# The four overhanging key columns of attention: the product with V issued over 128 rows instead of 4

## The chip, the cores and the metric

The kernel runs on one core of one Trainium2 chip. The metric is device time in microseconds (us), the median of several runs. TensorE (PE) multiplies matrices; VectorE (DVE), ScalarE (ACT) and GpSimd (POOL) work on rows; SyncE (SP) issues DMA transfers.

## The reference

The block is a half feed-forward, attention, and another half feed-forward, on x of 8 batches x 512 tokens x 256. Only attention matters here. Everything is float32:

```python
q, k, v = heads(x @ Wq), heads(x @ Wk), heads(x @ Wv)     # 16 heads of 64
k = concatenate([mem_k, k]); v = concatenate([mem_v, v])  # 4 memory keys ahead
dots = einsum('bhid,bhjd->bhij', l2norm(q), l2norm(k)) * 10
dots = einsum('hg,bgij->bhij', W_pre_th, dots)            # heads are mixed
dots = where(causal, mask_value, dots)
vk = top_k(dots, 64)[0][..., -1:]
dots = where(dots < vk, mask_value, dots)                 # the 64 largest stay
attn = softmax(dots)
attn = einsum('hg,bgij->bhij', W_post_th, attn)           # heads are mixed again
out = einsum('bhij,bhjd->bhid', attn, v) * head_scale * sigmoid(x @ Wg + bg)
x = x + out @ Wo
```

A row of `dots` has 516 columns: four memory keys and 512 tokens. So the keys that a tile of 128 queries can see are a whole number of 128-column blocks plus four more columns.

## The kernel before

Attention is `attention_phase`. A **tile** t is 128 queries; a batch has four tiles (TPB = 4), so there are 32. A tile is worked in 16 **groups** n of 8 queries: 8 queries x 16 heads fill 128 partitions, and a group's width in columns grows from 12 to 516 over the batch. Every engine walks its own hand-written list in steps of two groups (n0 = 0, 2, 4, ...), and semaphores tie the lists together.

What happens to group n, by engine:

- PE `score` makes the products of queries and keys, ACT copies them to SC (L1242), SP moves them by DMA to raw, PE `mix(n)` multiplies with mixpre (L1037), ACT `evict(n)` copies to S (L1253, L1256).
- POOL masks (L1388), ACT counts (L1263), POOL makes the threshold `minus_thr` (L1397), DVE `row_max` applies it (L1510) and `select_pair` picks the 64th largest and zeroes the rest of E (L1523 to L1568).
- POOL makes R from mixpost and rinv (L1413). PE `turn(n)` multiplies E with R (L1053) three steps later (LAG = 6 groups), ACT `out_PT(n)` copies the result to PT (L1289).
- Once a half tile u (64 queries, 8 groups) is there, PE `attend(u, pairs)` multiplies V with PT (L1079, one product for each head and each block of 128 keys), pair by pair of heads.

**The tail.** Behind the last whole block stand the four overhanging key columns. Only the second half tile (hh = 1) needs them, and of it the last eight queries. `turn` makes them at the last group of a tile (L1059, a result of 4 partitions), `out_PT` copies them to PTtail (L1294, 4 x 128), and `attend` adds for each of the 16 heads one product of 4 rows of V and 4 x 8 of PTtail (L1085).

**Where the tails stand in PE's list.** PE works the tails of tile t during tile t+1, second half: at g = 8 three pairs of heads, at g = 10 three, at g = 12 two. Ahead of the first stands `project(t - 1)` (L1099). The last tile's 16 heads come in one piece at the end, ahead of the last two projections. Each pair's list reads: L1079 products (1 to 4 blocks, two heads), L1085 products (two heads), next pair.

V has five slots of 128 keys in its ring. The four rows of the tail are the first four of slot t+1, which holds the keys of the next tile. A product in float32 shows in the trace as two LDWEIGHTS and two MATMUL records, so L1085's 512 products are 1024 records. The two heads of a pair write partitions 0 to 63 and 64 to 127.

Of the kernel before, what the change touches and what calls it, by code (L numbers as in the profile page):

```python
# [11 lines left out]
H, DH, MEM, TOPK = 16, 64, 4, 64  # L12
CYCLES = 3
P = 128
TPB = N // P
TILES = B * TPB
IG = 8
# [694 lines left out]
def attention_phase(nc, W, token_weights, a, x_dram, out_dram, again):  # L712

    with ExitStack() as c:
        def sb(name, shape, dtype=F32):
            return c.enter_context(nc.sbuf_tensor(name, shape, dtype))

        def sem(name):
            return c.enter_context(nc.semaphore(name))
# [3 lines left out]
        V = sb("V", [P, TPB + 1, HD])  # L723
# [36 lines left out]
        flag = sb("flag", [P, B])  # L760
        R = [sb(f"R{i}", [P, P]) for i in range(RBUFS)]
        PT = [sb(f"PT{i}", [P, TPB, H, HALF]) for i in range(2)]
        PTtail = sb("PTtail", [MEM, H, IG])

        def bank(name):
            return c.enter_context(nc.psum_tensor(name, [P, 512], F32))
# [5 lines left out]
        bankT = bank("bankT")  # L772
# [35 lines left out]
        rn_ready = sem("rn_ready")  # L808
        qk_ready = sem("qk_ready")
        halo = sem("halo")  # L810
        tk = sem("tk")
        flagged = sem("flagged")
        flag_sum = sem("flag_sum")
# [38 lines left out]
        def slot(j):  # L852

            return j % (TPB + 1)
# [55 lines left out]
        def wait_read(eng, *u):  # L910

            eng.wait_ge(D_read, max(place[x] for x in u) + 1)
# [54 lines left out]
        def _(pe):  # L967
# [95 lines left out]
            def attend(u, pairs):  # L1063
                t, hh = divmod(u, 2)
                if pairs[0] == 0:
                    pe.wait_ge(PT_out, (u + 1) * IG)
                    if t % TPB == 0:
                        pe.wait_ge(mem_in, 16 * (t // TPB + 1))
                        wait_read(pe, ("v", t, 1))
                    if hh:  # L1070
                        wait_read(pe, ("w", t, 1) if t == NT - 1 else ("v", t + 1, 1))
                    if u:
                        pe.wait_ge(gated, u)
                blocks = t % TPB + 1
                for pair in pairs:
                    for jb in range(blocks):
                        for lo in range(2):
                            h = 2 * pair + lo
                            last = nc.tensor.matmul(bankM[64 * lo:64 * lo + 64, pair * HALF:(pair + 1) * HALF],  # L1079
                                                    V[:, slot(t - blocks + 1 + jb), h * DH:(h + 1) * DH], PT[u % 2][:, jb, h, :],  # L1080
                                                    start=jb == 0, stop=jb == blocks - 1, skip_group_check=True)
                    if hh:
                        for lo in range(2):
                            h = 2 * pair + lo
                            last = nc.tensor.matmul(  # L1085
                                bankM[64 * lo:64 * lo + 64, (pair + 1) * HALF - IG:(pair + 1) * HALF],
                                V[0:MEM, slot(t + 1), h * DH:(h + 1) * DH], PTtail[:, h, :],
                                start=False, stop=True, skip_group_check=True)
                if pairs[-1] == PAIRS - 1:
                    last.then_inc(attended, 1)  # L1090
# [19 lines left out]
            for n0 in range(0, NG + LAG, 2):  # L1110
                t, g = divmod(n0, GPT)
# [47 lines left out]
                if t and g % 8 < 6:  # L1159
                    attend(2 * t - 2 + g // 8, ((0, 1, 2), (3, 4, 5), (6, 7))[g % 8 // 2])  # L1160
            attend(NU - 1, range(PAIRS))
            project(NT - 2)
            project(NT - 1)
# [4 lines left out]
        def _(act):  # L1168
# [113 lines left out]
            def out_PT(n):  # L1282
                t, g = divmod(n, GPT)
                u = n // IG
                act.wait_ge(turned, n + 1)
                if n % IG == 0 and u >= 2:
                    act.wait_ge(attended, u - 1)
                blocks, at = t % TPB + 1, n % IG * IG
                last = nc.scalar.copy(PT[u % 2][:, 0:blocks, :, at:at + IG],  # L1289
                                      bankC[n % 2][:, 0:blocks * P].rearrange("p (j h i) -> p j h i", h=H, i=IG))  # L1290
                if g == GPT - 1:
                    if t:
                        act.wait_ge(attended, 2 * t)
                    last = nc.scalar.copy(PTtail[:, :, :], bankT[0:MEM, 0:P].rearrange("p (h i) -> p h i", i=IG))  # L1294
                last.then_inc(PT_out, 1)

            xT(0)
# [6 lines left out]
            for n0 in range(0, NG + LAG, 2):  # L1304
                t, g = divmod(n0, GPT)
# [24 lines left out]
                if n0 >= LAG:  # L1330
                    out_PT(n0 - LAG)
                    out_PT(n0 + 1 - LAG)
# [26 lines left out]
        def _(pool):  # L1359

            def ln_rstd(j):
                pool.wait_ge(xn_stats, j + 1)
                nc.gpsimd.tensor_tensor(rstd[:, :], mv[:, 1:2], W.neghalf[:, 0:1], ALU.pow).then_inc(xn_rstd, 1)

            def copy_halo(j):

                dst = xnT[j % 2][:, :, 0:MEM]
                if j >= 2:
                    wait_read(pool, ("v", j - 2, 1))
                if j == 0:  # L1370
                    nc.gpsimd.memset(dst, 0.0).then_inc(halo, 1)
                else:
                    wait_read(pool, ("xT", j - 1, 0))
                    nc.gpsimd.tensor_copy(dst, xnT[1 - j % 2][:, :, P:P + MEM]).then_inc(halo, 1)

            def norm(j, i):
                pool.wait_ge(ssq_done, 2 * j + i + 1)
                nc.gpsimd.tensor_tensor(rn[:, i, :], ssq[:, i, :], W.neghalf[:, 0:H], ALU.pow).then_inc(rn_ready, 1)  # L1378
                pool.wait_ge(rn_ready, 2 * j + i + 1)
                wait_read(pool, ("qk"[i], j, 1))  # L1380
                v = qk[:, i, :].rearrange("p (h d) -> p h d", d=DH)
                nc.gpsimd.tensor_tensor(v, v, rn[:, i, :].unsqueeze(2).to_broadcast([P, H, DH]),
                                        ALU.mult).then_inc(qk_ready, 1)
# [31 lines left out]

            ln_rstd(0)
            copy_halo(0)
            norm(0, 0)
            norm(0, 1)
            ln_rstd(1)  # L1420
            for n0 in range(0, NG + LAG, 2):
                t, g = divmod(n0, GPT)
# [1039 lines left out]
def build(nc, a, out):  # L2462


    x1_dram = nc.dram_tensor("x1", ((TILES + 1) * P, D), F32, kind="Internal").ap()
    x2_dram = nc.dram_tensor("x2", (TILES * P, D), F32, kind="Internal").ap()
    rows = "b n d -> (b n) d"
    with ExitStack() as ctx:
        W = Weights()
        place_weights(nc, ctx, W)  # L2470
        names = ("Wq", "Wk", "Wv", "Wg")
        token_weights = [ctx.enter_context(nc.sbuf_tensor(n, [P, 2, HD], F32)) for n in names]
        with nc.sbuf_tensor("X_first", [P, TILES, D], F32) as X, ExitStack() as own:
            place_wide_weights(nc, own, W, "first", a)
            setup = Setup(nc, own, W, {**a, "x": a["x"].rearrange(rows)}, x1_dram)
            ffn_phase(nc, "ffn1", X, W, None, x1_dram, setup,
                      [(w[:, :, :], a[n].rearrange("(k p) n -> p k n", p=P)) for w, n in zip(token_weights, names)])
        again = ctx.enter_context(nc.sbuf_tensor("again", [P, B], I32))
        attention_phase(nc, W, token_weights, a, x1_dram, x2_dram, again)
        redo_phase(nc, W, token_weights, a, x1_dram, x2_dram, again)  # L2480
        with nc.sbuf_tensor("X_last", [P, TILES, D], F32) as X, ExitStack() as own:
            ffn_phase(nc, "ffn2", X, W, x2_dram, out.rearrange(rows), reload=place_wide_weights(nc, own, W, "last", a))
# [31 lines left out]
```

## Time and profile before

| | us |
|---|---|
| median of 3 runs | 2308.27 |
| lowest, highest | 2300.52, 2308.93 |
| span of the profiled execution | 2304.0 |
| PE busy in it | 2083.4 (90%) |
| DVE busy | 1767.9 (77%) |
| ACT busy | 1605.5 (70%) |
| POOL busy | 930.2 (40%) |

The profiled execution's own time is its span, first to last instruction, 2304.0; it lies 4.3 below the median of the three runs and between the lowest and the highest. Busy shares are averages over the whole span: the feed-forward parts take a little over 200 us at its start and as much at its end, and attention with its eight batches lies between. In the rows below, a time is counted from the span's start, a duration in square brackets at a row's end is idle time just before it with what ended it, and `x4` is a count of records.

### The profile page before, as it was taken

How to read it: one execution, taken by the hardware profiler on the slowest of the kernel's cores; microseconds unless marked ns; L12 is line 12 of the kernel's file. 1: busy time of each engine (PE TensorE's matmuls, PEld its weight loads, DVE VectorE, ACT ScalarE, POOL GpSimd, SP SyncE). 2: the span in 40 equal slices, each digit the busy share in tenths (PEclk: the TensorE clock that was granted, in tenths of full speed). 3: DMA queues.
4: the chain of work that ended last, by engine and by line, in shares of the span. 5: the costliest groups of instructions: out<-in, count | busy, mean ns of one | idle time of the engine just before them, and what ended most of it. 6: DMA issues, size and time to landing. Idle time of an engine off the chain costs nothing. (4 is left out here: it accounts for less than half of the span.)

```text
span 2304.0 us, 55635 instructions
## 1 busy us (share of the span) xinstructions
PE 2083.4 (90%) x16059; PEld 1351.7 (59%) x16060; DVE 1767.9 (77%) x6818; ACT 1605.5 (70%) x4676; POOL 930.2 (40%) x2738
## 2 busy tenths in 40 slices
PE   7995799989999999899989998999899989974997
PEld 3433456666666666666666666666666666663433
DVE  6565389958996899689968995899589958983446
ACT  4442589858985898689858976897689768851543
POOL 3001454444544554555455435543554355321000
PEclk9997799999999999999999999999999999997998
DMA  6002112111211121112111211121112101212002
GB/s 179 0 0 87 24 39 62 44 26 44 62 44 26 44 62 44 26 44 62 44 26 44 62 44 26 44 62 44 26 44 62 44 24 45 68 28 88 1 0 73
DMA packets 113219, 104.72 MB, mean 45 GB/s; under 512 B 34448, under 2 KB 110864, under 8 KB 112912
## 3 DMA queue, kind: packets, MB, share of 16 engines
q1 hardware_dynamic: 108000, 96.65, 16.5%
q10 hardware_dynamic: 4912, 4.46, 0.6%
q8 instruction: 134, 2.20, 0.4%
q14 instruction: 173, 1.42, 0.2%
HBM read 19.14 MB, written 12.71 MB: 14 GB/s over the span
## 5 line engine op out<-in xcount | busy, mean ns | idle before, releaser
L1053 PE MATMUL bankC<-R,E 128*128 128x128 f32 x2560 | 349.0, 286 | 39.5 <-POOL R L1413 39.4
L1053 PEld LDWEIGHTS bankC<-R,E 128*128 128x128 f32 x2560 | 335.6, 200 | 76.7 <-POOL R L1413 43.8
L1037 PE MATMUL bankB<-raw,mixpre 128*128 128x76 f32 (+37 forms) x1024 | 353.6, 433 | 18.9 <-DMA raw<-SC 18.6
L1388 POOL TENSOR_TENSOR S<-S,diagmask 128x8 f32<-128x8 f32 x512 | 114.2, 227 | 493.3 <-ACT S L1253 435.3
L1253 ACT ACTIVATE S<-bankB,aim_first 128x68 f32<-128x68 f32 (+56 forms) x456 | 231.5, 512 | 116.3 <-PE bankB L1037 115.6
L1510 DVE TENSOR_SCALAR_CACHE_REDUCE S<-S,minus_thr 128x68 f32<-128x68 f32 (+56 forms) x456 | 217.6, 514 | 110.1 <-POOL minus_thr L1397 109.5
L1564 DVE SCALAR_TENSOR_TENSOR E<-S,limit,E 128x68 f32<-128x68 f32 (+56 forms) x456 | 242.6, 567 | 35.4 <-ACT E L1279 6.3
L1413 POOL TENSOR_SCALAR R<-mixpost,rinv 128x128 f32<-128x128 f32 x512 | 187.5, 379 | 137.2 <-DVE rinv L1568 136.7
L1279 ACT ACTIVATE E<-S,nmax 128x12 f32<-128x12 f32 (+56 forms) x512 | 241.3, 533 | 0.0
L1079 PEld LDWEIGHTS bankM<-PT,V 128*64 128x64 f32 x5120 | 177.7, 137 | 101.1 <-issue 90.5
L1026 PE MATMUL bankD<-KT,QT 64*64 64x132 f32 (+8 forms) x2304 | 190.5, 405 | 51.2 <-ACT SC L1242 25.7
L1037 PEld LDWEIGHTS bankB<-raw,mixpre 128*128 128x128 f32 x1024 | 159.4, 191 | 118.8 <-issue 81.9
L1079 PE MATMUL bankM<-PT,V 128*64 128x64 f32 x5120 | 226.3, 229 | 0.9 <-DVE gate L1494 0.9
L1289 ACT COPY PT<-bankC 128x512 f32<-128x512 f32 (+3 forms) x512 | 193.9, 431 | 35.3 <-PE bankC L1053 30.3
L1271 ACT ACTIVATE junk_side<-S 128x68 bf16<-128x68 f32 (+56 forms) x456 | 199.5, 445 | 13.1 <-DVE S L1510 13.1
L1538 DVE MATCH_REPLACE8 near<-top,near 128x68 f32<-128x68 f32 (+56 forms) x456 | 199.5, 443 | 0.0
L1263 ACT ACTIVATE junk_first<-S 128x60 bf16<-128x60 f32 (+56 forms) x456 | 197.3, 444 | 0.3
L1378 POOL TENSOR_TENSOR rn<-ssq,neghalf 128x16 f32<-128x16 f32 x64 | 187.5, 2930 | 12.2 <-DVE ssq L1486 12.0
L1533 DVE MAX8 top<-near 128x8 f32<-128x68 f32 (+56 forms) x456 | 186.9, 449 | 0.3
L1542 DVE MAX8 top<-near 128x8 f32<-128x68 f32 (+56 forms) x456 | 186.3, 447 | 0.3
L1242 ACT COPY SC<-bankD 128x136 f32<-128x136 f32 (+7 forms) x256 | 165.8, 647 | 22.4 <-PE bankD L1026 20.5
L1528 DVE TENSOR_SCALAR near<-S,flip 128x68 int32<-128x68 int32 (+56 forms) x456 | 155.6, 381 | 8.2
(177 smaller groups left out, 3915.0 us busy)
## 6 DMA issues: line engine op xcount, KB each, us to landing
X_first<-in_L_attn_x_dram ACTq DMA_DIRECT2D x8, 512.0 KB, 10.1
x<-X_first SPq DMA_DIRECT2D x8, 512.0 KB, 2.9
xt<-x SPq DMA_DIRECT2D x32, 128.0 KB, 2.4
x<-xt SPq DMA_DIRECT2D x32, 128.0 KB, 2.5
X_last<-x SPq DMA_DIRECT2D x8, 512.0 KB, 6.7
out_dram<-X_last SPq DMA_DIRECT2D x8, 512.0 KB, 2.8
raw<-SC SPq DMA_DIRECT2D x8, 258.0 KB, 3.0
raw<-SC SPq DMA_DIRECT2D x8, 254.0 KB, 3.4
```

The source lines that it names most:

```text
L1026: last = nc.tensor.matmul(bankD[cols, r, i * s[3]:(i + 1) * s[3]], QT[rows, pair, HALF * hh:HALF * hh + HALF], KT[rows, pair, first:first ...
L1037: last = nc.tensor.matmul(bankB[n % 2][:, 0:wide(n)], W.mixpre[:, :], raw[n % RAWS][:, 0:wide(n)], start=True, stop=True)
L1053: last = nc.tensor.matmul(bankC[n % 2][:, jb * P:(jb + 1) * P], E[n % EBUFS][:, jb * P:(jb + 1) * P], R[n % RBUFS][:, :], start=True, stop ...
L1079: last = nc.tensor.matmul(bankM[64 * lo:64 * lo + 64, pair * HALF:(pair + 1) * HALF], V[:, slot(t - blocks + 1 + jb), h * DH:(h + 1) * DH] ...
L1253: nc.scalar.activation(S[n % SBUFS][:, 0:wide(n)], src, ACT.Identity, bias=W.aim_first[:, group(n)]).then_inc(S_out, 1)
L1263: nc.scalar.activation(junk_first[n % 2][:, 0:w], S[n % SBUFS][:, 0:w], ACT.Sign, scale=-1.0, accum_out=below[:, col(n)]).then_inc(below_d ...
L1271: nc.scalar.activation(junk_side[n % 2][:, 0:w], S[n % SBUFS][:, 0:w], ACT.Sign, accum_out=signs[:, col(n)]).then_inc(signs_done, 1)
L1279: nc.scalar.activation(E[n % EBUFS][:, 0:w], S[n % SBUFS][:, 0:w], ACT.Exp, bias=nmax[:, col(n)]) \
L1289: last = nc.scalar.copy(PT[u % 2][:, 0:blocks, :, at:at + IG], bankC[n % 2][:, 0:blocks * P].rearrange("p (j h i) -> p j h i", h=H, i=IG))
L1510: nc.vector.tensor_scalar(row, row, minus_thr[:, col(n)], None, ALU.add, ALU.max, accum_out=rmax[:, col(n)]).then_inc(max_done, 1)
L1538: at[n] = step(nc.vector.match_replace(out=row, in_to_replace=top[n % 2][:, 8 * r - 8:8 * r], in_values=row, imm_value=-FMAX))
L1564: at[n] = step(nc.vector.scalar_tensor_tensor(out=E[n % EBUFS][:, 0:w], in0=S[n % SBUFS][:, 0:w], scalar=least, in1=E[n % EBUFS][:, 0:w], ...
```

## The change

PTtail gets 128 partitions instead of 4. POOL fills it with zeros once, before the first tile. ACT goes on writing its first four partitions, and waits for the zeros at the first tile. The tail's product is issued with all 128 rows of V's slot and all 128 of PTtail. Rows 4 to 127 of PTtail are never written again, so they add zero times a value of V. The number of products and of records is the same, and so is their order.

```diff
-        PTtail = sb("PTtail", [MEM, H, IG])
+        PTtail = sb("PTtail", [P, H, IG])
...
+        tail_rows_zero = sem("tail_rows_zero")
...
                             last = nc.tensor.matmul(
                                 bankM[64 * lo:64 * lo + 64, (pair + 1) * HALF - IG:(pair + 1) * HALF],
-                                V[0:MEM, slot(t + 1), h * DH:(h + 1) * DH], PTtail[:, h, :],
+                                V[:, slot(t + 1), h * DH:(h + 1) * DH], PTtail[:, h, :],
                                 start=False, stop=True, skip_group_check=True)
...
                     if t:
                         act.wait_ge(attended, 2 * t)
-                    last = nc.scalar.copy(PTtail[:, :, :], bankT[0:MEM, 0:P].rearrange("p (h i) -> p h i", i=IG))
+                    else:
+                        act.wait_ge(tail_rows_zero, 1)
+                    last = nc.scalar.copy(PTtail[0:MEM, :, :], bankT[0:MEM, 0:P].rearrange("p (h i) -> p h i", i=IG))
...
             ln_rstd(0)
             copy_halo(0)
+            nc.gpsimd.memset(PTtail[:, :, :], 0.0).then_inc(tail_rows_zero, 1)
             norm(0, 0)
```

The only list with a row more is POOL's, at the start of attention. Before, behind the last table of the set-up:

```order
L624 TENSOR_TENSOR spread<-spread,half 128x1
L77 UNCONDITIONAL_BRANCH
L1358 UNCONDITIONAL_BRANCH
L1363 TENSOR_TENSOR rstd<-mv,neghalf 128x1
L1371 MEMSET xnT 128x2x4
L1378 TENSOR_TENSOR rn<-ssq,neghalf 128x16
L1382 TENSOR_TENSOR qk<-qk,rn 128x1024
```

And now, with the lines shifted by the new ones:

```order
L1361 UNCONDITIONAL_BRANCH
L1366 TENSOR_TENSOR rstd<-mv,neghalf 128x1
L1374 MEMSET xnT 128x2x4
L1421 MEMSET PTtail 128x128
L1381 TENSOR_TENSOR rn<-ssq,neghalf 128x16
L1385 TENSOR_TENSOR qk<-qk,rn 128x1024
```

The fill of PTtail stands between the fill of xnT's first columns and the first norm; PE's list has the same products in the same order as before.

## Rows read from the trace of the kernel before

**Rows 1.** The page, busy time of each engine.
```profile
PE 2083.4 (90%) x16059; PEld 1351.7 (59%) x16060; DVE 1767.9 (77%) x6818; ACT 1605.5 (70%) x4676; POOL 930.2 (40%) x2738
```

**Rows 2.** PE groups by shape: busy us, mean ns, then idle before.
```profile
L1079 PE MATMUL bankM<-PT,V 128*64 128x64 f32 x5120 | 226.3, 229 | 0.9 <-DVE gate L1494 0.9
L1085 PE MATMUL bankM<-PTtail,V 4*64 4x8 f32 x1024 | 72.6, 208 | 0.0
```

**Rows 3.** Timeline of PE, a run of L1079 without tails (tile 16, first half).
```profile
1147.85 1.62 PE L1079 MATMUL bankM<-PT,V 128*64 128x64 f32 x48
1149.39 0.41 PE L1037 MATMUL bankB<-raw,mixpre 128*128 128x28 f32 x2
```

**Rows 4.** Timeline of PE, three pairs with tails (tile 15, second half).
```profile
1117.51 0.57 PE L1079 MATMUL bankM<-PT,V 128*64 128x64 f32 x12
1118.00 0.28 PE L1085 MATMUL bankM<-PTtail,V 4*64 4x8 f32 x4
...
1119.64 0.67 PE L1037 MATMUL bankB<-raw,mixpre 128*128 128x476 f32 x1
```

**Rows 5.** Windows of tiles 16 to 19, half by half; PEclk is PE's granted clock.
```profile
1139.40:1177.40 38.00, 32.62 (x290) 23.21 (x291) 23.86 (x81) 18.41 (x55) 19.65 (x38) 0.91 0.06 15
1177.40:1197.40 20.00, 18.24 (x254) 14.93 (x252) 11.98 (x79) 13.37 (x63) 8.30 (x36) 1.00 0.07 17
1197.40:1225.80 28.40, 25.53 (x168) 15.81 (x167) 22.07 (x111) 21.73 (x80) 18.02 (x42) 1.00 0.21 54
1225.80:1249.30 23.50, 23.38 (x187) 16.87 (x185) 21.47 (x110) 19.60 (x68) 9.66 (x39) 1.00 0.21 53
1249.30:1276.50 27.20, 26.38 (x204) 16.73 (x203) 25.52 (x101) 25.45 (x79) 18.71 (x40) 1.00 0.25 61
1276.50:1304.90 28.40, 28.40 (x230) 19.17 (x229) 27.14 (x110) 24.71 (x68) 10.33 (x38) 1.00 0.23 53
1304.90:1338.70 33.80, 32.20 (x285) 20.13 (x285) 32.43 (x113) 30.49 (x80) 18.95 (x41) 1.00 0.30 72
1338.70:1367.20 28.50, 26.09 (x270) 20.15 (x268) 26.35 (x90) 25.52 (x67) 9.32 (x34) 0.99 0.14 31
```

**Rows 6.** Waits in 1177.4:1197.4 (first two) and 1225.8:1367 (last two).
```profile
DVE S L1510 <- POOL minus_thr L1397: 6.9, 3, 3.7
PE bankB L1037 <- DMA raw<-SC: 1.8, 1, 1.8
...
DVE S L1510 <- POOL minus_thr L1397: 1.8, 3, 0.7
PE bankD L1026 <- ACT SC L1242: 2.0, 3, 1.3
```

**Rows 7.** Timeline of PE where batches meet; the last row is one batch earlier.
```profile
1140.78 3.30 PE L1053 MATMUL bankC<-R,E 128*128 128x128 f32 x16 [3.71 <-POOL R L1413]
...
1161.55 5.37 PE L985 MATMUL bankD<-Wv,xnT 128*128 128x512 f32 x8 [0.58 <-ACT SC L1242]
...
934.95 3.67 PE L985 MATMUL bankD<-Wv,xnT 128*128 128x512 f32 x8 [0.58 <-ACT SC L1242]
```

**Rows 8.** Timeline of DVE, its waits in tiles 15 and 17, second halves.
```profile
1115.06 0.69 DVE L1510 TENSOR_SCALAR_CACHE_REDUCE S<-S,minus_thr 128x460 f32<-128x460 f32 x1 [0.35 <-POOL minus_thr L1397]
...
1124.21 0.71 DVE L1510 TENSOR_SCALAR_CACHE_REDUCE S<-S,minus_thr 128x476 f32<-128x476 f32 x1 [0.72 <-POOL minus_thr L1397]
...
1236.04 0.44 DVE L1510 TENSOR_SCALAR_CACHE_REDUCE S<-S,minus_thr 128x220 f32<-128x220 f32 x1 [0.72 <-POOL minus_thr L1397]
```

**Rows 9.** Timeline of PE, the last tile's `attend`, eight pairs in one piece.
```profile
2070.40 0.69 PE L1079 MATMUL bankM<-PT,V 128*64 128x64 f32 x16 [0.94 <-DVE gate L1494]
...
2077.02 3.72 PE L1099 MATMUL bankT<-Wo,gate 128*128 128x256 f32 x16
```

**Rows 10.** POOL: timeline at attention's start, and a fill of the same size.
```profile
219.76 2.91 POOL L1378 TENSOR_TENSOR rn<-ssq,neghalf 128x16 f32<-128x16 f32 x1 [9.93 <-DVE ssq L1486]
...
L595 POOL MEMSET ident<- 128x128 f32 x1 | 0.2, 205 | 0.3 <-POOLq L2503 0.3
```

## The prediction, made before the changed kernel was run

> **What bounds the kernel now.** I read the page first. PE is busy 90% of the span, DVE 77%, ACT 70% [rows 1]. That makes PE the suspect, but it is an average. So I cut one batch (tiles 16 to 19) into half tiles with the windows view [rows 5], and asked in each half who waits for whom [rows 6]. The reader is to see three regimes:
>
> - *Tile 16, first half* (1139.4 to 1177.4): nobody is full. PE waits 3.71 us for R, so for DVE, which is still finishing the widest groups of the batch before [rows 7].
> - *Tile 16, second half, and tile 17, first half* (20.0 and 28.4 us): DVE is busy 11.98 of 20.0, PE 18.24 of 20.0. DVE waits 6.9 us, always at L1510, for a threshold that hangs on S and so on PE's `mix` [rows 6]. PE's list sets the pace here.
> - *Tile 17, second half, to the end of tile 19* (141.4 us): PE looks full, 28.40 of 28.40 in one half, but so is DVE: 27.14 of 28.40, 32.43 of 33.80, 25.52 of 27.20 [rows 5]. What is missing to 100% is not waiting: in all 141.4 us DVE waits 1.8 us in three places at L1510 [rows 6]. So here DVE is the limit, and PE keeps up with it without a wait of any size (2.0 us for SC). At the end of the stretch PE stands still for 3.71 us and DVE does not. A faster PE gains in this stretch no more than DVE's waits, and the rest comes back as a longer wait at 1140.78.
>
> **The price of a tail on PE.** Mean durations mislead: a 4-row product shows 208 ns, a 128-row one 229 ns [rows 2], and both overlap their neighbours. Starts do not mislead. In a run of 48 L1079 records the next group starts 1149.39 - 1147.85 = 1.54 us later [rows 3]; a run of 12 ahead of a tail takes 1118.00 - 1117.51 = 0.49 us [rows 4]. Two equations, records times P plus a fixed D: P = (1.54 - 0.49) / 36 = 0.0292 us a record, D = 0.49 - 12 x 0.0292 = 0.14 us at the end of a run. Three pairs with tails take 1119.64 - 1117.51 = 2.13 us, 0.71 each, so the four tail records take 0.71 - 0.49 = 0.22, of which 4 x 0.0292 = 0.12 would be records at L1079's pace. I read D, and the 0.10 behind the tail, as the price of going between products of 128 rows and of 4. L1079's next head has other weights too and pays nothing, so it is not the weights.
>
> **The change, part by part.**
>
> - *The product over 128 rows.* No trace of before shows one with 8 moving columns over 128 rows. From below: its weights are L1079's (128 x 64) and its moving columns fewer, so P = 0.029 a record, or a little less. From above: if a run also ends for some other reason (another source tile, 8 columns for 64), four records cost 4 x 0.0292 + 0.14 = 0.26, 0.04 more than today. I take P: in rows and weights the product equals L1079, to which it is nearest, and differs only in columns.
> - *What that saves.* A pair with three blocks goes from 0.71 to 16 x 0.0292 = 0.47 us, 0.24 saved, whatever the number of blocks. Each run keeps one D at its end. So three pairs save 3 x 0.243 - 0.14 = 0.59, two pairs 0.35, and a tile 0.59 + 0.59 + 0.35 = 1.53 us. The last tile's eight pairs take 2077.02 - 2070.40 = 6.62 us [rows 9] and would take 160 x 0.0292 + 0.14 = 4.81: 1.81 saved. Over the whole kernel PE is relieved of 31 x 1.53 + 1.81 = 49.2 us.
> - *What of it lies on the path.* The tails worked in tiles 4, 8, ..., 28 (seven times) stand in the PE-bound stretch: all 1.53 counts, because the scores, their copy, the DMA to raw (PE waits 1.8 us for it [rows 6]) and the next `mix` all move up together: 7 x 1.53 = 10.7. Those in tiles 5, 9, ..., 29 stand where DVE has just become the limit; at 1236.04 it still waits 0.72 us, after the first three pairs [rows 8], so their 0.59 counts: 7 x 0.59 = 4.1. Those in tiles 6, 10, ... meet no wait of DVE; they give PE a lead. With it DVE's waits of 0.35 and 0.72 in tile 15 [rows 8], which stand again in the same places of the other batches, should vanish in tiles 3, 7, ..., 27: 7 x 1.07 = 7.5. The last tile's 1.81 lies bare: DVE has nothing to do but wait for bankM. Sum 10.7 + 4.1 + 7.5 + 1.8 = 24.1 us, half of what PE is relieved of.
> - *The zeros.* A fill of 128x128 took 0.2 us, and POOL idles 9.93 us just behind the place where it goes [rows 10]. Nothing. Without that cover it would be 0.2 us once.
> - *ACT's new wait* comes at the last group of the first tile, for a fill that POOL does before that tile's first norm; ACT's copy stays one of 4 partitions. Nothing queues behind it. The wait at the other tiles is the old one.
> - *Slower work elsewhere*: none is added. SP's transfers are the same; those to raw start when SC and a buffer are ready, a little earlier where PE is earlier.
>
> A rule bears on this. The Trainium skill, page "TensorE: Matmul & The Clock Gate", section "LDWEIGHTS (loading the stationary operand)", says that a load's time goes by its columns and not by its rows, so 32 rows and 128 take the same. The records' lengths agree roughly (208 and 229 ns [rows 2]). Taken alone it would make the change worth nothing, since only rows change. Starts speak against that: 0.22 us for four narrow records, 0.12 for four wide ones. By the rule the time is 2308 (as in rival 2), by the rows 2284.
>
> **The sum.** The profiled span of 2304.0 becomes 2304.0 - 24.1 = 2279.9. It was 4.3 below the median of the three runs; carried to the median, 2308.27 - 24.1 = 2284.2. I forecast **2284 us**.
>
> **The rivals.**
>
> 1. *PE's relief counts in full.* 49.2 us, 2259. It would need DVE to have hidden slack in tiles 2 and 3 of a batch. Against it: 27.14 busy of 28.40 with no wait [rows 5, 6]. For it: PE busy 28.40 of 28.40 in the same half.
> 2. *The runs end anyway.* A tail costs 0.26 for 0.22, 0.04 x 8 x 32 = 10 us of PE time, half of it on the path: 5, so 2308 to 2313, no change that can be told. For it: no row shows 8 columns over 128 rows. Against: nothing else in the trace explains D.
> 3. *Only the bare places gain.* If PE's lead is used up by R (it may not turn a group before DVE has finished it), or the waits at L1510 hang on ACT's order of work and not on PE, what remains is 10.7 + 1.8 = 12.5 us: 2296, at the edge of what can be told.
> 4. *Slower, by PE's clock.* PE will idle more: per batch some 3 x 1.53 - 1.66 = 2.9 us come back as waits (1.66 is what the batch gains in tiles 1 to 3). After the wait of 3.71 us the granted clock falls (a mean of 0.91 in that half [rows 5]); it is the lower of the two levels, 1.2 GHz, in part of it. What that costs shows one `tokens`: 3.67 us for Wv a batch earlier, 5.37 here [rows 7], 1.7 us. If the added waits fall in tiles 17 to 19, where the clock is 1.00 now and PE has no slack, each such stretch costs 1.7 us. To end 11.5 us slower than before, 24 + 11.5 = 36 us must go, so 21 stretches, three for each of seven batches. Against it: the extra wait should join the one at 1140.78, where PE works ahead of DVE anyway. By the section "HAM oscillation" of the same page of the Trainium skill, idle gaps between bursts make the clock fall, and it must be expected in every batch; by the rows tiles 17 to 19 run at 1.00 or 0.99 in spite of their small waits [rows 5, 6], and a stretch can be won as well as lost: the batch with 3.67 did not pay it.
>
> Shifts of that clock also set my own range: one stretch of 1.7 us more or less in each of seven batches is 12 us, so 2272 to 2296 for the likeliest case.
>
> **How the numbers follow.** Chances: the likeliest case 0.62, rival 1 0.07, rival 2 0.13, rival 3 0.12, rival 4 0.06. A measurement of this kernel tells about 0.5%, 11.5 us, from no change. Faster: 0.60 + 0.07 + 0.05 = 0.72. Same: 0.02 + 0.13 + 0.07 = 0.22. Slower: 0.06. The range reaches from rival 1 to rival 3 with the likeliest case's clock between: 2258 to 2300, which leaves out rivals 2 and 4, 0.19.
>
> **What would show it.** On PE's timeline the tail's products start 0.03 us apart in one run with L1079's, and three pairs of tile 15's kind take 1.5 us, not 2.13. Half tile 16b takes 18.5, not 20.0. DVE's waits at L1510 in tiles 17 to 19 fall from 1.8 us to about 0.1. PE's wait for R at the batch's start grows from 3.71 to 5 or more. The last `attend` takes 4.8, not 6.62. Wrong would make me: a D between L1079 and the padded product, halves of tiles 18 and 19 that get shorter than DVE's busy time allows, or a clock below 1.00 in tiles 17 to 19.

## The result, and the profile after

| | before | changed |
|---|---|---|
| median of 5 runs, us | 2303.7 | 2284.8 |
| span of the profiled execution, us | 2304.0 | 2285.0 |

The ratio is 0.991, with a 95% interval of 0.989 to 0.993, so the change makes the kernel 19 us faster. Two further runs of the kernel before brought its median down from the 2308.3 that the forecast started from. One execution of the changed kernel (6275.5 us) and one of the kernel of run 4 (6749.4 us) took almost three times as long as the others; the ratios leave them out, and without them the medians are 2284.6 here and 2294.4 in run 4. When the changed kernel ran again on another occasion the ratio was 0.990 (0.987 to 0.993).

The page of the changed kernel, busy time of each engine; compare [rows 1]:

```profile
PE 2040.8 (89%) x16059; PEld 1325.7 (58%) x16060; DVE 1765.2 (77%) x6818; ACT 1602.4 (70%) x4676; POOL 938.0 (41%) x2739
```

PE has as many records as before and is busy 43 us less. DVE has the same count and nearly the same busy time. PE's groups by shape, busy us, mean ns and idle before, answering to [rows 2] (L1079 is now L1080, L1085 is L1086):

```profile
L1080 PE MATMUL bankM<-PT,V 128*64 128x64 f32 x5120 | 211.2, 228 | 0.9 <-DVE gate L1498 0.9
...
L1086 PE MATMUL bankM<-PTtail,V 128*64 128x8 f32 x1024 | 61.4, 189 | 0.0
```

The tail's mean length fell by a tenth, from 208 to 189 ns, which says little. The starts say it. PE's timeline at the place of [rows 4], three pairs of tile 15:

```profile
1111.34 0.57 PE L1080 MATMUL bankM<-PT,V 128*64 128x64 f32 x12
1111.74 0.24 PE L1086 MATMUL bankM<-PTtail,V 128*64 128x8 f32 x4
1111.83 0.55 PE L1080 MATMUL bankM<-PT,V 128*64 128x64 f32 x12
1112.21 0.24 PE L1086 MATMUL bankM<-PTtail,V 128*64 128x8 f32 x4
...
1112.84 0.67 PE L1038 MATMUL bankB<-raw,mixpre 128*128 128x476 f32 x1
```

Four tail records now take 0.09 us from start to next start (1111.74 to 1111.83) instead of 0.22, and the 12 ahead of them 0.37 to 0.40 instead of 0.49. Three pairs take 1.50 us instead of 2.13. The last `attend` of the kernel, where [rows 9] showed 6.62 us:

```profile
2053.04 0.69 PE L1080 MATMUL bankM<-PT,V 128*64 128x64 f32 x16 [0.95 <-DVE gate L1498]
...
2057.80 3.72 PE L1100 MATMUL bankT<-Wo,gate 128*128 128x256 f32 x16
```

That is 4.76 us. The windows of tiles 16 to 19, cut like [rows 5] where ACT takes the first group of each half tile from bankB; the columns are length, busy time of PE, PEld, DVE, ACT and POOL, PE's granted clock, DMA share and GB/s:

```profile
1131.90:1169.20 37.30, 31.73 (x290) 23.23 (x291) 24.73 (x84) 18.50 (x56) 19.69 (x38) 0.91 0.07 16
1169.20:1187.80 18.60, 16.84 (x254) 14.19 (x252) 11.85 (x79) 13.35 (x64) 8.36 (x36) 0.98 0.09 21
1187.80:1217.20 29.40, 26.86 (x169) 16.86 (x168) 22.30 (x114) 21.91 (x81) 18.18 (x42) 0.95 0.19 51
1217.20:1239.60 22.40, 21.69 (x186) 15.78 (x185) 20.92 (x107) 19.41 (x68) 10.05 (x39) 1.00 0.21 54
1239.60:1266.80 27.20, 26.38 (x204) 16.73 (x203) 25.52 (x103) 25.45 (x79) 18.81 (x40) 1.00 0.26 63
1266.80:1294.00 27.20, 26.76 (x230) 18.15 (x230) 25.97 (x104) 24.52 (x68) 9.38 (x37) 1.00 0.23 53
1294.00:1330.50 36.50, 34.01 (x287) 21.42 (x286) 35.10 (x121) 30.57 (x81) 19.57 (x42) 0.95 0.28 70
1330.50:1357.60 27.10, 24.42 (x270) 19.12 (x268) 24.33 (x83) 25.24 (x67) 9.05 (x34) 1.00 0.12 28
```

Every second half, where the tails stand, is shorter: 18.6 for 20.0, 22.4 for 23.5, 27.2 for 28.4, 27.1 for 28.5. But two first halves are longer, 29.4 for 28.4 and 36.5 for 33.8, and just these two show a granted clock of 0.95 where [rows 5] had 1.00. Of the 5.1 us that the second halves won, 3.7 went there. One such stretch, seen closely, right behind the wait for raw ahead of tile 17:

```profile
1187.20:1190.40 3.20, 3.20 (x12) 2.46 (x12) 3.13 (x21) 2.28 (x13) 1.53 (x7) 0.50 0.55 149
```

The granted clock is 0.50, the lower of PE's two levels, 1.2 GHz instead of 2.4. The 29.4 us of that half tile are the mild case: the same half tile takes 29.3 to 31.8 us in the batches after the first. The profile lists such a stretch at the start of the second tile in all seven batches after the first; in the kernel before in three. So the first question for the runs was whether PE's price and place were read rightly, and the second what the clock took.

### The profile page after: what moved, and what is told of

The parts are those of the page before. It is cut to its first block and busy times, and to the rows that moved or that the text cites. A ratio compares the mean times of both kernels' runs of the same rounds, so it can differ in the third digit from the quotient of the medians.

```text
span 2285.0 us, 55636 instructions
## 1 busy us (share of the span) xinstructions
PE 2040.8 (89%) x16059; PEld 1325.7 (58%) x16060; DVE 1765.2 (77%) x6818; ACT 1602.4 (70%) x4676; POOL 938.0 (41%) x2739
## 5 line engine op out<-in xcount | busy, mean ns | idle before, releaser
L1514 DVE TENSOR_SCALAR_CACHE_REDUCE S<-S,minus_thr 128x68 f32<-128x68 f32 (+56 forms) x456 | 217.7, 514 | 94.1 <-POOL minus_thr L1400 93.5
L1568 DVE SCALAR_TENSOR_TENSOR E<-S,limit,E 128x68 f32<-128x68 f32 (+56 forms) x456 | 234.1, 549 | 37.6 <-ACT E L1280 9.0
L1080 PEld LDWEIGHTS bankM<-PT,V 128*64 128x64 f32 x5120 | 180.3, 138 | 97.9 <-issue 90.5
L1290 ACT COPY PT<-bankC 128x512 f32<-128x512 f32 (+3 forms) x512 | 195.0, 435 | 34.3 <-PE bankC L1054 29.3
L1080 PE MATMUL bankM<-PT,V 128*64 128x64 f32 x5120 | 211.2, 228 | 0.9 <-DVE gate L1498 0.9
```

Of the source, the lines that this page charges most:

```text
L1514: nc.vector.tensor_scalar(row, row, minus_thr[:, col(n)], None, ALU.add, ALU.max, accum_out=rmax[:, col(n)]).then_inc(max_done, 1)
L1568: at[n] = step(nc.vector.scalar_tensor_tensor(out=E[n % EBUFS][:, 0:w], in0=S[n % SBUFS][:, 0:w], scalar=least, in1=E[n % EBUFS][:, 0:w], ...
```

## The experiments

All ratios are to the kernel before, measured beside each kernel on the same chip. The medians of runs 1 to 4 belong together, those of 5 to 8, and those of 9 to 12; a difference between two of these sets also holds what separates one occasion from another, and the kernel before had 2305.4, 2305.6 and 2304.6 us in them.

**1. 64 rows instead of 128.** Is it the step between row counts that costs, or does a narrow product get better with each row?

```diff
-        PTtail = sb("PTtail", [P, H, IG])
+        PTtail = sb("PTtail", [64, H, IG])
...
-                                V[:, slot(t + 1), h * DH:(h + 1) * DH], PTtail[:, h, :],
+                                V[0:64, slot(t + 1), h * DH:(h + 1) * DH], PTtail[:, h, :],
```

> The padding goes to 64 rows instead of 128: PTtail has 64 partitions, and the product takes the first 64 rows of V. Theory (what costs is going between products of 128 rows and of fewer): on PE's timeline three pairs with three blocks take 2.1 us as with 4 rows, the four tail records 0.2 us, and the time is that of before, ratio 0.997 to 1.003. Rival (a narrow product is slow by itself and more rows make it quicker step by step): three pairs between 1.63 and 2.1 us, ratio between 0.991 and 0.998.

Measured: 2304.9 us, ratio 1.0003 (0.9988 to 1.0019). PE's timeline at the same three pairs:

```profile
1117.13 0.57 PE L1080 MATMUL bankM<-PT,V 128*64 128x64 f32 x12
1117.63 0.28 PE L1086 MATMUL bankM<-PTtail,V 64*64 64x8 f32 x4
1117.85 0.57 PE L1080 MATMUL bankM<-PT,V 128*64 128x64 f32 x12
...
1119.27 1.88 PE L1038 MATMUL bankB<-raw,mixpre 128*128 128x476 f32 x4
```

2.14 us, within a hundredth of what 4 rows cost. Sixteen times as many rows bring nothing; of the three row counts that were run only the full 128 helps. The rival falls.

**2. Four rows, but the tails behind one another.** The kernel before, with the tail's loop moved out of the loop over pairs:

```diff
                 for pair in pairs:
...
-                    if hh:
-                        for lo in range(2):
+                if hh:
+                    for pair in pairs:
+                        for lo in range(2):
                             h = 2 * pair + lo
                             last = nc.tensor.matmul(
...
                                 V[0:MEM, slot(t + 1), h * DH:(h + 1) * DH], PTtail[:, h, :],
```

> The kernel before with its 4-row products, but the tails of all pairs of one call of attend stand behind its last pair, so there are 3 runs of tails a tile instead of 8. Theory (each going over costs about 0.24 us there and back): three pairs with three blocks take 36 x 0.0292 + 0.14 + 12 x 0.03 + 0.10 = 1.6 to 1.7 us instead of 2.13, the last attend 5.2 to 5.3 instead of 6.62, and the ratio to before is 0.991 to 0.995, nearly that of the change. Rival (it is the 4 rows of a product that cost, wherever it stands): 2.13 us stays, ratio 1.000.

Measured: 2284.7 us, ratio 0.992 (0.9905 to 0.9938): as fast as the change as far as the intervals tell, with no row more. PE's timeline, three pairs:

```profile
1106.57 1.27 PE L1079 MATMUL bankM<-PT,V 128*64 128x64 f32 x36
1107.77 0.52 PE L1086 MATMUL bankM<-PTtail,V 4*64 4x8 f32 x12
1108.22 1.88 PE L1037 MATMUL bankB<-raw,mixpre 128*128 128x476 f32 x4
```

1.65 us, and the last `attend` takes 4.92 instead of 6.62. (The 5.2 to 5.3 expected for it was a slip: the expectation's own terms give 128 x 0.0292 + 0.14 + 32 x 0.03 + 0.10 = 4.94.) A narrow record in a run costs about as little as a wide one: 12 take 0.45 us with the end of the run in it. What costs is the step from 128 rows to fewer and back, 0.24 us a pair. The Trainium skill, page "TensorEngine Tiling (Array Packing)", section "Key Properties", states that changing the tiling mode, not just the tile, drains TensorE. By that rule 4 and 64 rows are alike foreign to a product of 128, and the trace agrees (2.13 and 2.14 us), though no row shows the drain itself. That section of the Trainium skill gives no price; the rows do.

**3 and 4. Where the relief counts.** 128 rows only for the tails of each batch's last tile (8 of 32), and only for the other 24:

```diff
+                tail_rows = P if t % TPB == TPB - 1 else MEM
...
-                                V[:, slot(t + 1), h * DH:(h + 1) * DH], PTtail[:, h, :],
+                                V[0:tail_rows, slot(t + 1), h * DH:(h + 1) * DH], PTtail[0:tail_rows, h, :],
```

(in the fourth run `t % TPB < TPB - 1`).

> 128 rows only for the tails of each batch's last tile (worked in the half tile where PE sets the pace, and the one at the kernel's end); the other 24 tiles keep 4-row products over the same PTtail. Theory (only where DVE waits does PE's relief count): 7 x 1.53 + 1.81 = 12.5 us less, ratio 0.9945, less what the clock takes back; the measured change gave only 0.8 us in the half tiles concerned instead of 1.5, which would make 7.3 us, ratio 0.997. Rival (relief counts alike everywhere): a quarter of 19 us, 4.8 us, ratio 0.998.

> The opposite part: 128 rows for the tails of the first three tiles of each batch, 4 rows for the last tile's. Theory (in these stretches DVE is the limit and only its waits are won): 4.1 + 7.5 = 11.6 us less, ratio 0.995. Rival (relief counts alike everywhere): three quarters of 19 us, 14 us, ratio 0.994; rival (the gain was all in the half tiles where PE sets the pace): ratio 1.000.

Measured: 2295.2 us, ratio 0.9956 (0.9939 to 0.9972), and 2294.4 us, ratio 0.9956 (0.9938 to 0.9975). Eight tails give 10.2 us, the other 24 give 11.0 by the medians, and by the ratios both give about 10. So one of the eight tails (seven in the stretch where PE sets the pace, one at the kernel's end) is worth about three times one elsewhere. The third run's trace has the half tile of the seven at 18.3 to 18.9 us and leaves the others at their old lengths. That relief counts alike everywhere is out by the third run (4.8 us expected, 6.4 the least that its interval holds); the fourth alone would just allow 14 us. That all came from the PE-bound stretch is out too.

**5 and 6. The change again, and its zeros alone.** The sixth kernel is the change with the product back at `V[0:MEM, ...]` and `PTtail[0:MEM, ...]`.

> The changed kernel once more, beside the three others of this call. All theories: ratio to before 0.991, within 0.002.

> The change without its widened product: PTtail has 128 partitions, POOL zeroes it, ACT waits for that once, and the product takes 4 rows as before. Theory (zeros and wait are hidden): ratio 1.000, within 0.002. Rival (the place or the zeroing of the larger tile matters): more than 0.002 from 1.

Measured: ratio 0.990 (0.987 to 0.993), and 0.9997 (0.998 to 1.0014). The larger tile, its fill and ACT's wait are free, as far as 0.2% can tell.

**7. No tails at all.** The tail's products are left out, and with them the four overhanging keys' share of the output.

> The changed kernel with the tail's products left out altogether (the four overhanging keys are missing from the output of the last eight queries of each tile). PE is relieved of another 4 x 0.0225 us a pair, 0.72 us a tile, 23 us in all. Theory (about 0.4 of PE's relief shows, as 19 of 49 us did): 9 us less than the change, ratio to before 0.987. Rival (DVE's waits and the clock have taken all there was): same as the change, ratio 0.991. Rival (PE was still the limit everywhere): ratio 0.981.

Measured: 2272.2 us, ratio 0.985 (0.982 to 0.987); 11.6 us below the change measured beside it (2283.8). I expected 9. Half of what is taken from PE shows, not 0.4 of it. PE's relief has not run dry.

**8 to 12. The clock.** These kernels give PE products that nobody reads, in places where it stands still anyway:

```diff
+            def fill(count):
+                for _ in range(count):
+                    nc.tensor.matmul(bankT[:, 136:232], W.ident[:, :], W.mixpre[:, 0:96], start=True, stop=True)
...
                 if live:
+                    if g == 0 and t % TPB == 1:
+                        fill(7)
                     mix(n0)
...
                     if g == 4:
+                        if t % TPB == 0 and t:
+                            fill(12)
                         score(2 * t + 1, 1)
```

The eighth kernel is the change with both; the ninth the kernel before with both; the tenth the change with only `fill(7)`; the eleventh with only `fill(12)`; the twelfth has both and a third, in `score`:

```diff
                 for s in score_steps(u, q):
+                    if s[2] == "last":
+                        fill(6)
```

> The changed kernel with products that nobody reads, put where PE stands still in its trace: 7 of 96 columns (about 1.1 us) ahead of the wait for raw at the start of each batch's second tile (PE idle 1.8 to 2.0 us there), and 12 (about 1.9 us) ahead of the wait for the k projection in the first tile of batches 1 to 7 (idle 2.8 us). Theory (what the change lost again is the granted clock falling at these two waits): the clock stays 1.00 behind them, the first half of each second tile goes from 29.3 to 30.1 back to about 28.4 us, the first half of a first tile loses 1.7 us in five or six of seven batches, and the ratio to before is 0.985 to 0.988. Rival (the clock falls in spite of them, or does not matter): 0.991, or above it if the products cost more than the idle time.

> The kernel before with the same unread products in the same two places as in the run with both fills on the changed kernel (2266.9 us, ratio 0.9824), so that the clock is held behind both waits in either kernel and the difference between the two is the change alone. Theory (per batch 1.66 us where PE sets the pace and 1.95 us in the rest, seven batches, and 1.8 us at the end, 27 us; the clock took the rest back): this kernel lies 25 to 29 us above 2266.9, at 2292 to 2296, ratio to before 0.994 to 0.996. Rival (the clock has no part in the change's result): 19 to 21 us above, 2286 to 2288, ratio 0.992.

> The changed kernel with only the 7 products ahead of the wait for raw at each second tile. Theory: the clock stays up in the first half of the second tiles (28.4 us instead of 29.3 to 30.1, seven times, some 8 us), while first halves of first tiles still take 39.0 us in most batches; ratio 0.9865 to 0.988. Rival (both places are needed, since the fall moves to the other): 0.990.

> The changed kernel with only the 12 products ahead of the wait for the k projection in the first tiles. Theory: first halves of first tiles take 37.3 to 37.9 us in all batches (five of seven took 39.0, some 8 us less), second tiles keep their 29.3 to 30.1; ratio 0.986 to 0.988. Rival (as above): 0.990.

> The changed kernel with both fills and a third: 6 products (1.0 us) ahead of the 4-column score products of the fourth tile's second half, where PE waits 0.4 and 1.3 us for ACT and the clock falls in four of seven batches with both fills. Theory: the first half of every fourth tile takes 34.5 instead of 36.1 to 36.5 us, four times, 7 to 8 us less than with two fills; 2259 to 2261 us, ratio 0.979 to 0.980. Rival (the products delay ACT's copies there by as much): 2267 us, ratio 0.982.

| kernel | median us | ratio to before | interval |
|---|---|---|---|
| change, both fills | 2266.9 | 0.9824 | 0.9797 to 0.985 |
| before, both fills | 2292.6 | 0.9942 | 0.9923 to 0.9962 |
| change, 7 ahead of raw | 2266.3 | 0.983 | 0.9808 to 0.9852 |
| change, 12 ahead of k | 2269.8 | 0.9846 | 0.982 to 0.9871 |
| change, three fills | 2265.2 | 0.9824 | 0.9802 to 0.9847 |

The seven products of the tenth kernel, and what is left of the wait behind them, on PE's timeline:

```profile
1177.66 1.70 PE L1095 MATMUL bankT<-mixpre,ident 128*128 128x96 f32 x14
1179.62 0.51 PE L1038 MATMUL bankB<-raw,mixpre 128*128 128x140 f32 x2 [0.25 <-DMA raw<-SC]
```

PE does the same useful work at the same time, with 1.7 us of waiting replaced by work. The kernel with both fills, measured beside the change, is 16.8 us faster (2266.9 against 2283.8; I had expected a ratio of 0.985 to 0.988 and got 0.982). The one with the fill ahead of raw alone is 38 us faster than the kernel before and 17.5 us below the change's 2283.8, which was taken on the other occasion. I had expected 8 for its seven batches.

That expectation took the stretch at half clock for too cheap. In the tenth kernel's trace it is gone in all eight batches: the first half of the second tile takes 28.3 to 28.8 us, where the change's trace has 29.3 to 31.8, and summed over the eight batches that is 12.2 of the 18.7 us between the two profiled executions. None is left in the fourth tiles either, where the two profiles of the change had two and four and where nothing was added. A first half of a first tile still shows 39.0 to 39.3 us in four batches, 37.3 to 37.5 in three.

But the eighth kernel, which has this fill too, shows the fall again in four of its fourth tiles (36.1 to 36.4 us for 34.5), so one profile of each can't tell whether the fill clears that place or the falls wander from execution to execution. The eleventh kernel missed its expectation in another way: it adds nothing at the second tiles, and yet of the seven batches after the first only two still fall there (30.1 and 30.5 us; 28.3 to 28.8 in the others). So the places are not independent, and the sum of parts that I had expected is wrong: either fill alone gets most. In the twelfth kernel's trace the fourth tiles are clear in all seven batches (34.6 to 35.0 us), but its time was expected at 2259 to 2261 us and is 2265.2, not clearly below the kernels with one fill ahead of raw or two. How a fill reaches another place I have not shown.

The ninth kernel answers the main question. The two fills take 12.0 us off the kernel before (2304.6 to 2292.6) and 16.8 off the change. With the fills in both kernels the change is worth 2292.6 - 2266.9 = 25.7 us across two occasions (27 by the two ratios, 0.9942 and 0.9824); without them 19 to 22 (18.9 and 21.9 on the two occasions that had both kernels). The intervals of these ratios reach 4 to 6 us to either side, and those of the two differences overlap, so the times alone do not show that the clock took part of the change's worth. One profile of each points the same way: from the start of tile 4 to the start of tile 28 it is 1372.2 us before and 1364.4 with the fills, but 1357.3 with the change and 1344.1 with the change and its fill ahead of raw, so the fills win 7.8 in one and 13.2 in the other.

For the clean view, one batch of each without a fall in the places that count (they are not the same batch, and only the first has the fill ahead of k). First the kernel before with both fills, tiles 16 to 19:

```profile
1134.60:1171.20 36.60, 33.97 (x314) 25.74 (x315) 23.93 (x81) 18.47 (x55) 19.64 (x38) 0.92 0.07 16
1171.20:1191.20 20.00, 19.75 (x268) 16.50 (x266) 11.98 (x79) 13.36 (x63) 8.25 (x36) 1.00 0.07 17
1191.20:1219.50 28.30, 25.64 (x169) 15.89 (x168) 22.09 (x112) 21.80 (x81) 18.14 (x42) 1.00 0.20 52
1219.50:1242.90 23.40, 23.28 (x186) 16.78 (x185) 21.41 (x109) 19.49 (x68) 9.62 (x39) 1.00 0.21 54
...
1270.10:1298.40 28.30, 28.30 (x229) 19.07 (x228) 27.04 (x109) 24.59 (x67) 10.37 (x38) 1.00 0.22 51
1298.40:1332.30 33.90, 32.31 (x286) 20.22 (x285) 32.54 (x113) 30.57 (x80) 18.93 (x41) 1.00 0.30 74
1332.30:1360.80 28.50, 26.08 (x270) 20.16 (x268) 26.36 (x90) 25.51 (x67) 8.99 (x34) 1.00 0.12 28
```

Then the change with the fill ahead of raw, tiles 20 to 23:

```profile
1347.30:1384.60 37.30, 31.84 (x290) 23.25 (x291) 24.73 (x84) 18.50 (x55) 19.64 (x38) 0.91 0.07 16
1384.60:1403.00 18.40, 18.17 (x268) 15.52 (x266) 11.74 (x77) 13.37 (x63) 8.28 (x36) 1.00 0.08 20
1403.00:1431.50 28.50, 25.57 (x168) 15.86 (x167) 22.36 (x115) 21.79 (x80) 18.02 (x42) 1.00 0.21 53
1431.50:1453.90 22.40, 21.69 (x185) 15.79 (x184) 20.87 (x107) 19.41 (x67) 9.63 (x39) 1.00 0.21 53
...
1481.10:1508.30 27.20, 26.75 (x230) 18.14 (x229) 25.94 (x107) 24.52 (x67) 9.95 (x38) 1.00 0.22 51
1508.30:1542.80 34.50, 32.38 (x286) 20.25 (x285) 33.14 (x114) 30.45 (x80) 19.49 (x42) 1.00 0.30 73
1542.80:1569.90 27.10, 24.48 (x270) 19.17 (x268) 25.88 (x87) 25.24 (x66) 9.80 (x34) 1.00 0.14 31
```

The reader is to go down the first numbers: +0.7, -1.6, +0.2, -1.0, (27.2 in both), -1.1, +0.6, -1.4; sum 226.2 against 222.6. The half tiles with tails win 5.1 us, and 1.5 come back in three first halves. In the largest, the +0.7, PE's wait for R grew from 3.8 to 4.7 us, a wait for DVE; what holds the other two I have not shown. A batch is worth 3.6 us net, of which 1.4 in the half tile where PE alone sets the pace and 2.2 in the rest.

## Why the prediction was right, point by point

- **What bounds the kernel.** Held. Runs 3 and 4 show both regimes: 10.2 us from a quarter of the tails, 11.0 from the rest, for 12.5 and 11.6 forecast.
- **The price of a tail** from starts, P = 0.0292 and D = 0.14. Held, and a little better than forecast: the padded record takes 0.0225, below the lower bound's 0.029, so three pairs took 1.50 us (forecast 1.54) and the last `attend` 4.76 (4.81). That D belongs to the change of row count was an inference; runs 1 and 2 show it.
- **1.53 us a tile where PE sets the pace.** 20.0 us became 18.4 to 18.6: held, in place and size.
- **DVE's waits as the measure of the rest.** Held in part. I had forecast that the 1.8 us of waits at L1510 (now L1514) in tiles 17 to 19 would fall to about 0.1. In tiles 16 to 19 they come to 2.0: the steps of [rows 8] shrank, but a wait of 1.59 stands behind the fourth tile's stretch at half clock.

```profile
1226.85 0.44 DVE L1514 TENSOR_SCALAR_CACHE_REDUCE S<-S,minus_thr 128x220 f32<-128x220 f32 x1 [0.22 <-POOL minus_thr L1400]
...
1334.61 0.69 DVE L1514 TENSOR_SCALAR_CACHE_REDUCE S<-S,minus_thr 128x460 f32<-128x460 f32 x1 [1.59 <-POOL minus_thr L1400]
...
1343.26 0.71 DVE L1514 TENSOR_SCALAR_CACHE_REDUCE S<-S,minus_thr 128x476 f32<-128x476 f32 x1 [0.22 <-POOL minus_thr L1400]
```

  In tiles 20 to 23, whose fourth tile has no such stretch, two are left, 0.6 in all:

```profile
1454.58 0.44 DVE L1514 TENSOR_SCALAR_CACHE_REDUCE S<-S,minus_thr 128x220 f32<-128x220 f32 x1 [0.29 <-POOL minus_thr L1400]
...
1560.80 0.69 DVE L1514 TENSOR_SCALAR_CACHE_REDUCE S<-S,minus_thr 128x460 f32<-128x460 f32 x1 [0.27 <-POOL minus_thr L1400]
```

  The two batches of the clean view show the same, 1.8 us against 0.6. So 1.2 of the 1.66 us was won at these waits, while the rest of a batch gave 2.2. A wait of 0.5 at the line that zeroes E is gone as well; the remainder is open.
- **The sign that I was wrong.** I had named a clock below 1.00 in tiles 17 to 19. It is there: 0.95 in the first halves of tiles 17 and 19. [Rows 5] showed a batch without it; other batches of the kernel before have it too, only fewer. That the added idle time would only lengthen the wait for R, where it harms nobody, did not hold.
- **The surplus comes back as a wait for R.** In direction only: I had forecast 3.71 growing to 5 or more. It was 3.79 at tile 16, with a new wait of 1.25 us for raw just ahead, and 4.69 one batch earlier:

```profile
1129.62 0.39 PE L1038 MATMUL bankB<-raw,mixpre 128*128 128x12 f32 x2 [1.25 <-DMA raw<-SC]
...
1134.27 3.78 PE L1054 MATMUL bankC<-R,E 128*128 128x128 f32 x16 [3.79 <-POOL R L1416]
```

- **The zeros and the wait.** Free: the fill took 0.23 us ahead of a wait of 10.24, and run 6 shows no difference.

```profile
210.27 0.23 POOL L1421 MEMSET PTtail<- 128x128 f32 x1
220.74 2.91 POOL L1381 TENSOR_TENSOR rn<-ssq,neghalf 128x16 f32<-128x16 f32 x1 [10.24 <-DVE ssq L1490]
```

- **The sum, 24.1 us.** The change gave 19 in the first comparison and 22 in the second. The term that I had left at zero is the clock's. I had written of it as a spread of 12 us either way around nothing, and as rival 4. Its mechanism is in the trace, at the start of the second and in the fourth tiles, but it took some 4 to 7 us by the differences of the medians, not 36, and these 4 to 7 lie within the intervals. With the fills in both kernels the change is worth 25.7; the sum lies between the two. That the forecast of 2284 hit the median of 2284.8 within 1 us is luck, since the kernel before was also 4.6 us quicker, at 2303.7, than the median that I started from.
- **The rivals.** Rival 1 (all 49 us) is out: 25.7 at best (27 by ratios, give or take 8). Rival 2 (runs end anyway) is out by the timeline. Rival 3 (only the bare places gain) is out by run 4. Rival 4 (slower) is out by the ratio. The rule of the Trainium skill on loads, page "TensorE: Matmul & The Clock Gate", section "LDWEIGHTS (loading the stationary operand)", agrees roughly with the trace as a rule on loads: the loads last 130 ns with 4 rows and with 64, 138 with 128. It says nothing of what the neighbours cost, and there the change won. (The 208 and 229 ns that the prediction set beside it are of the products, not of the loads.)

## What to carry to other kernels

Look at the starts of small products on TensorE, not at their lengths: two equations from runs of different length give the price of a record and the price of ending a run. If a narrow product stands between products of 128 rows, either pad it with zeros to the same rows or gather the narrow ones in one run; here both gave the same 20 us. And look at the granted clock behind PE's waits: a few unread products in waits that are there anyway took 12 us off the kernel before and 17 off the change, nearly as much again as the change itself.

## What the runs showed of the hardware that I had not expected

- 64 rows cost the same as 4 beside 128-row products: 2.14 and 2.13 us for three pairs, 1.50 with 128 rows.
- Products with 8 columns over 128 rows start 0.0225 us apart, below the 0.0292 of those with 64 columns and the same weights' size.
- Seven unread products of 96 columns (1.7 us in a wait of about 2 us), issued once in each of the eight batches, left the whole kernel 17.5 us below the change. Of the 18.7 us between the two profiled executions 12.2, 1.5 a batch, lie in the half tile behind this wait, the rest elsewhere. The Trainium skill, page "TensorE: Matmul & The Clock Gate", section "HAM oscillation", warns that waits between bursts of products let the clock fall; here the fall came behind this wait of 1.8 to 2.0 us in every batch after the change and went away when the wait was filled. But the wait alone does not decide it: in the kernel before, five of the batches after the first have the same 1.8 us there and the clock fell in two of them, and a wait of 2.65 us in another was followed by no fall. Why it falls more often after the change is open.
- The best of all kernels were the change with the fill ahead of raw, alone or with others, 2265.2 to 2266.9 us, 38 to 39.5 us below the kernel before.
